# Low-rank terms of gate and up: from activations to the expanded weights

## What is computed

```python
def _lin_lora(x, W, A, B):
    base = jnp.einsum('bsh,oh->bso', x, W)
    lora = jnp.einsum('bsr,or->bso', jnp.einsum('bsh,rh->bsr', x, A), B)
    return base + lora
q, k, v = (_lin_lora(x, dequant(codes_attn[i], ...), lora_A_h[i], lora_B_attn[i]) for i in range(3))
attn = (q + k + v) / 3.0
x1 = x + _lin_lora(attn, dequant(codes_attn[3], ...), lora_A_h[3], lora_B_attn[3])
g = _lin_lora(x1, dequant(codes_gu[0], ...), lora_A_h[4], lora_B_gu[0])   # 1792 outputs
u = _lin_lora(x1, dequant(codes_gu[1], ...), lora_A_h[5], lora_B_gu[1])   # 1792 outputs
h = jax.nn.silu(g) * u
d = _lin_lora(h, dequant(codes_down, ...), lora_A_down, lora_B_down)
x = layernorm(x + x1 + d)
```

## Time and profile before

| | us |
|---|---|
| median of 3 runs | 562.48 (561.15 to 564.53) |
| the profiled execution's own time | 561.32 |
| its span on the core | 559.5 |
| TensorE busy | 495.7 (89%) |
| VectorE busy | 437.1 (78%) |
| ScalarE busy | 363.4 (65%) |
| GpSimd busy | 336.2 (60%) |
| mean granted clock | 0.966 |

### The profile page before, as it was taken

One profiled execution on the slowest core, in us unless ns is written; L12 is line 12 of the kernel. 1 busy time (PEld: TensorE's weight loads), 2 busy tenths in 40 slices (PEclk: granted clock), 3 DMA queues, 4 the chain that ended last, 5 costly groups with the idle time before them and its releaser, 6 DMA issues.

```text
span 559.5 us, 8029 instructions
## 1 busy us (share of the span) xinstructions
PE 495.7 (89%) x2246; PEld 399.0 (71%) x2246; DVE 437.1 (78%) x823; ACT 363.4 (65%) x657; POOL 336.2 (60%) x318
## 2 busy tenths in 40 slices
PE   0474549979799999999999999999999899999995
PEld 0152338767688888888888888778887688888874
DVE  7999988988868889999999999268646985555442
ACT  8999956688868578979889796126668541242121
POOL 5898824069866679989989899324649711010011
PEclk9996669989999999999999999999999999999999
DMA  8642402023322133333323230154000000010010
GB/s 268 247 147 75 132 19 68 15 89 134 97 90 77 57 94 105 104 95 111 116 94 114 94 100 15 56 198 151 2 1 1 1 2 1 19 39 21 0 39 37
DMA packets 20507, 43.70 MB, mean 78 GB/s; under 512 B 3312, under 2 KB 3440, under 8 KB 19952
## 3 DMA queue, kind: packets, MB, share of 16 engines
q1 hardware_dynamic: 20240, 42.81, 23.9%
q0 software_dynamic: 224, 0.38, 0.3%
HBM read 41.08 MB, written 2.10 MB: 77 GB/s over the span
## 4 chain that ended last, share of the span: by engine, by line
PE 68%; POOL 15%; issue 13%; ACT 2%; DVE 2%; POOLq 0%; ACTq 0%; DVEq 0%
PE bank L886 59%; POOL wf L623 6%; PE bank L1020 3%; POOL wf L631 3%; POOL wf L636 2%; PE bank L979 2%; POOL wf L642 2%; PE bank L1005 1%; PE bank L1124 1%; ACT prob L847 1%; ACT pT_hi L689 1%; PE bank L904 0%; DVE rmax L1335 0%; POOL wd_lo L649 0%; DVE pT_lo L1164 0%
## 5 line engine op out<-in xcount | busy, mean ns | idle before, releaser
L710 ACT ACTIVATE bank<-code 128x512 f32<-128x512 int32 x372 | 207.5, 594 | 18.7 <-DVE half L1183 7.7
L623 POOL TENSOR_TENSOR wf<-halves 128x512 f32<-128x512 f32 x62 | 80.2, 1294 | 69.3 <-DVE halves L1187 68.3
L886 PE MATMUL bank<-x_hi,gu_hi 128*128 128x512 f32 x224 | 88.4, 395 | 2.8 <-POOL gu_lo L649 2.2
L672 POOL TENSOR_TENSOR rstd<-veps,neg_half 128x1 f32<-128x1 f32 x32 | 17.7, 552 | 121.6 <-issue 110.4
L886 PE MATMUL bank<-x_hi,gu_lo 128*128 128x512 f32 x224 | 88.0, 393 | 0.0
L886 PE MATMUL bank<-x_lo,gu_hi 128*128 128x512 f32 x224 | 87.9, 392 | 0.0
L1183 DVE SCALAR_TENSOR_TENSOR half<-half,bank 128x512 f32<-128x512 f32 x124 | 81.2, 676 | 5.0 <-ACT bank L710 5.0
L1181 DVE SCALAR_TENSOR_TENSOR half<-code,bank 128x512 f32<-128x512 int32 x124 | 78.9, 676 | 5.2 <-ACT bank L710 3.8
L1187 DVE TENSOR_TENSOR halves<-half,bank 128x512 f32<-128x512 f32 x124 | 79.0, 677 | 0.0
L631 POOL TENSOR_TENSOR wf<-wf,scale 128x512 f32<-128x512 f32 x50 | 65.3, 1306 | 3.9
L886 PEld LDWEIGHTS bank<-x_hi,gu_hi 128*128 128x128 f32 x224 | 42.4, 189 | 12.3 <-issue 2.6
(11 more groups left out here) (199 smaller groups left out, 1130.5 us busy)
## 6 DMA issues: line engine op xcount, KB each, us to landing
code<-codes SPq DMA_DIRECT2D x62, 256.0 KB, 2.7
scale<-scales SPq DMA_DIRECT2D x100, 128.0 KB, 2.9
xs<-xT SPq DMA_DIRECT2D x1, 2048.0 KB, 11.8
ea_raw<-ex_A SPq DMA_DIRECT2D x1, 2048.0 KB, 9.7
eb_raw<-ex_B SPq DMA_DIRECT2D x1, 2048.0 KB, 7.7
out<-rows SPq DMA_DIRECT2D x8, 256.0 KB, 2.0
bgu_raw<-loB_gu SPq DMA_DIRECT2D x1, 1792.0 KB, 9.2
wqkv_raw<-w_qkv SPq DMA_DIRECT2D x1, 768.0 KB, 4.3
```

What stands on the lines that cost most here:

```text
L623: pool.tensor_tensor(w, halves[:, j % 2, 0, :], halves[:, j % 2, 1, :], ALU.subtract).then_inc(diff_done, 1)
L710: nc.scalar.activation(plane[m % RING_PLANE][:, :], src, func, bias=float(start), scale=float(slope)).then_inc(plane_ready, 1)
L886: last = nc.tensor.matmul(ps, a, b, start=start and i == 0 and n == 0, stop=stop and i == len(terms) - 1 and n == 2)
```

## The change

`MERGED` takes in the g and u chunks. For each of these TensorE makes the low-rank weight term A^T B as four matmuls of 128 moving columns (operands `la_gu` and `lb_gu`, float32r, with high and low parts stacked in the partitions), and VectorE adds it to `wf` ahead of the split, as for d chunks. The split of a g or u chunk is due after three halves where it was due after two. The product p, its two copies and splits, and the thirteenth matmul of each gate and up product go. The preparation of the operands is one high part of 128 x 1024 and one of 128 x 1792, with low parts over 32 partitions, where it was one of 128 x 512 and two of 128 x 1792; the transfers are 512 and 896 KB where they were 256 and 1792 KB. The orders of x1, of slice 0 and of TensorE's low-rank products are written anew: in TensorE's order of most slices f the product for the d chunk of f+1 is held back into the next slice, and those for g and u of f+1 stand behind the second and the third down product.

```diff
-MERGED = [c for c in CHUNKS if c[0] in "ovdf"]
+MERGED = [c for c in CHUNKS if c[0] not in "qk"]
...
-                due.append([3 if c in MERGED else 2, ("split", c)])
+                due.append([3, ("split", c)])
...
+    due.clear()
+    order += [("x1", 0), ("bprep", 0), ("x1", 1), ("bprep", 1), ("x1", 2)]
     half(("u", 0), 0)
-    order.append(("x1", 1))
+    order += [("x1", 3), ("merge", ("g", 0))]
     half(("u", 0), 1)
-    order += [("x1", 2), ("bprep", 0), ("x1", 3), ("bprep", 1), ("x1", 4), ("x1", 5), ("bprep", 2),
-              ("x1", 6), ("x1", 7)]
+    due.clear()
+    order += [("x1", 4), ("split", ("g", 0)), ("x1", 5), ("merge", ("u", 0)), ("x1", 6), ("split", ("u", 0)), ("x1", 7)]
     lut(("g", 1))
-    order.append(("p", 0))
     half(("u", 1), 0)
-    order.append(("p", 1))
...
 def tensor_order():
     order = []
+    held = ("d", 1)
     for f in range(NF):
-        downs = downs_beside(f)
+        downs = downs_beside(f) + [None] * 4
+        ahead = [(m, f + 1) for m in "gud"] if 1 <= f < NF - 1 else []
+        late = ("f", FFN_AT[f]) if f in FFN_AT else None
+        if f == 0:
+            beside = [None, ("u", 1), ("d", 0), None]
+        elif late:
+            beside = [ahead[0], ahead[1], ahead[2], None]
+        else:
+            beside = [held, *ahead[:2], None] if ahead else [held, None, None, None]
+        if late:
+            order.append(("lora", held))
         for b in range(NB):
             order.append(("gate", 2 * f + b))
-            if b == 0 and f < 2:
-                order.append(("lora", ("d", f)))
-            if b == 0 and f - 1 in FFN_AT:
-                order.append(("lora", ("f", FFN_AT[f - 1])))
-            order.extend(downs[2 * b:2 * b + 1])
+            if beside[2 * b] and not (late and b == 0) and not b:
+                order.append(("lora", beside[0]))
+            order.append(downs[2 * b])
+            if beside[2 * b] and (late and b == 0 or b):
+                order.append(("lora", beside[2 * b]))
             order.append(("up", 2 * f + b))
-            order.extend(downs[2 * b + 1:2 * b + 2])
-            if b == 0 and 1 <= f < NF - 1:
-                order.append(("lora", ("d", f + 1)))
+            order.append(downs[2 * b + 1])
+            if beside[2 * b + 1]:
+                order.append(("lora", beside[2 * b + 1]))
+        if f:
+            held = late or (ahead[2] if ahead else None)
     return order + downs_beside(NF)
...
-        bgu_raw = at("bgu_raw", 98, [P, 2, FF])
-        a4_raw = at("a4_raw", 112, [P, KT, P])
+        bgu_raw = at("bgu_raw", 98, [P, FF])
+        agu_raw = at("agu_raw", 105, [P, 2, 512])
...
-        bg4 = at("bg4", 134, [P, FF], F32R)
-        p4 = at("p4", 141, [P, TOK], F32R)
-        a4_hi = at("a4_hi", 205, [P, KT, P], F32R)
+        la_gu = at("la_gu", 134, [P, 2, 512], F32R)
...
                     act.wait_ge(bgu_in, 16)
-                    act.wait_ge(a4_in, 16)
+                    act.wait_ge(agu_in, 16)
                     act.wait_ge(weight_ready, 4 * KT)
-                    copy(*((a4_hi[:, :, :], a4_raw[:, :, :]), (bg4[:, :], bgu_raw[:, 0, :]),
-                           (bu4[:, :], bgu_raw[:, 1, :]))[i], bprep_hi)
+                    if i == 0:
+                        copy(la_gu[:, :, :], agu_raw[:, :, :], bprep_hi)
+                    else:
+                        copy(lb_gu[:, :], bgu_raw[:, :], bprep_hi)
...
-                elif kind == "p":
-                    b = item[1]
-                    act.wait_ge(p_ready, b + 1)
-                    copy(p4[:, b * SEQ:(b + 1) * SEQ], mm_ps[2 + b][:, :], phi_done)
...
+                elif kind in "gu":
+                    pe.wait_ge(bprep_done, 2)
+                    for h in range(KT):
+                        last = nc.tensor.matmul(lora_ps[:, h * P:(h + 1) * P],
+                                                la_gu[:, "gu".index(kind), h * P:(h + 1) * P],
+                                                lb_gu[:, k * P:(k + 1) * P], start=True, stop=True)
+                    last.then_inc(lora_ready, 1)
+                    return
...
-
-            pe.wait_ge(bprep_done, 3)
-            for b in range(NB):
-                pe.wait_ge(x1hi_done, NB * KT - 1 + b)
-                pe.wait_ge(x1lo_done, NB * KT - 1 + b)
-                pe.wait_ge(xs_done, NB * KT - 1 + b)
-                tk = slice(b * SEQ, (b + 1) * SEQ)
-                product(mm_ps[2 + b][:, :], [(a4_hi[:, k, :], a4_lo[:, k, :], x1_hi[:, k, tk], x1_lo[:, k, tk])
-                                             for k in range(KT)]).then_inc(p_ready, 1)
+                if n in (3, 5, 7):
+                    lora((("g", 0), ("u", 0), ("g", 1))[n // 2 - 1])
 
             def unit(n, g):
 
                 f, b = n // NB, n % NB
                 m = 2 * n + g
                 tk = slice(b * SEQ, (b + 1) * SEQ)
-                if m == 2:
-                    pe.wait_ge(phi_done, NB)
-                    pe.wait_ge(plo_done, NB)
+                if m <= 2:
+                    seen = (KT + 1, KT + 2, NB * KT)[m]
+                    pe.wait_ge(x1hi_done, seen)
+                    pe.wait_ge(x1lo_done, seen)
+                    pe.wait_ge(xs_done, seen)
                 elif m > 2 and g == 0:
                     pe.wait_ge(h_done, n - 1)
                 elif m > 2:
@@ -973,11 +978,7 @@
                 pe.wait_ge(lo_done, split_no(("gu"[g], f)))
                 s, ps = f % RING_GU, unit_ps[m % 3][:, :]
                 product(ps, [(gu_hi[:, s, g, k, :], gu_lo[:, s, g, k, :], x1_hi[:, k, tk], x1_lo[:, k, tk])
-                             for k in range(KT)], stop=False)
-                pe.wait_ge(phi_done, min(n + 1, NB))
-                pe.wait_ge(plo_done, min(n + 1, NB))
-                nc.tensor.matmul(ps, (bg4, bu4)[g][:, f * P:(f + 1) * P], p4[:, tk], start=False, stop=True)\
-                    .then_inc((gate_ready, unit_ready)[g], 1)
+                             for k in range(KT)]).then_inc((gate_ready, unit_ready)[g], 1)
 
...
-                    dve.wait_ge(low_rows_set, 4)
                     if i == 0:
-                        low(a4_lo[:, :, :], a4_raw[:, :, :], a4_hi[:, :, :], bprep_done)
+                        low(la_gu[32:64, :, :], agu_raw[32:64, :, :], la_gu[32:64, :, :], bprep_done)
                     else:
-                        b4 = (bg4, bu4)[i - 1]
-                        nc.vector.scalar_tensor_tensor(b4[:, :], b4[:, :].bitcast(F32), low_rows[:, 0:1],
-                                                       bgu_raw[:, i - 1, :], ALU.mult, ALU.add)\
-                            .then_inc(bprep_done, 1)
+                        low(lb_gu[64:96, :], bgu_raw[64:96, :], lb_gu[64:96, :], bprep_done)
...
-                elif kind == "p":
-                    b = item[1]
-                    tk = slice(b * SEQ, (b + 1) * SEQ)
-                    dve.wait_ge(phi_done, b + 1)
-                    low(p4[64:128, tk], mm_ps[2 + b][64:128, :], p4[64:128, tk], plo_done)
...
+    la_gu = np.zeros((P, 2, 512), np.float32)
+    lb_gu = np.zeros((P, FF), np.float32)
+    for i in range(3):
+        for g in range(2):
+            r = 32 * i + RANK * g
+            la_gu[r:r + RANK, g] = Ah[4 + g]
+            lb_gu[r:r + RANK] = Bg[g].T
```

More of the change, by code:

```diff
@@ L145, in vector_order @@
     half(("g", 0), 1)
-    order.append(("x1", 0))
+    due.clear()
+    order += [("x1", 0), ("bprep", 0), ("x1", 1), ("bprep", 1), ("x1", 2)]
     half(("u", 0), 0)
-    order.append(("x1", 1))
+    order += [("x1", 3), ("merge", ("g", 0))]
     half(("u", 0), 1)
-    order += [("x1", 2), ("bprep", 0), ("x1", 3), ("bprep", 1), ("x1", 4), ("x1", 5), ("bprep", 2),
-              ("x1", 6), ("x1", 7)]
+    due.clear()
+    order += [("x1", 4), ("split", ("g", 0)), ("x1", 5), ("merge", ("u", 0)), ("x1", 6), ("split", ("u", 0)), ("x1", 7)]
     lut(("g", 1))
-    order.append(("p", 0))
     half(("u", 1), 0)
-    order.append(("p", 1))
     order.append(("dprep", 0))
@@ L305, in build @@
         lb_qkv = at("lb_qkv", 192, [3 * RANK, 512])
-        bu4 = at("bu4", 194, [P, FF], F32R)
+        lb_gu = at("lb_gu", 194, [P, FF], F32R)
         la_d = at("la_d", 30, [P, FF // 2])
@@ L311, in build @@
         lb_dhi = at("lb_dhi", 82, [P, 2, 512], F32R)
-        a4_lo = at("a4_lo", 132, [P, KT, P], F32R)
         ident = at("ident", 207, [P, P])
@@ L395, in build @@
         bgu_in = sem("bgu_in")
-        a4_in = sem("a4_in")
+        agu_in = sem("agu_in")
         plane_ready = sem("plane_ready")
@@ L421, in build @@
         fprep_done = sem("fprep_done")
-        p_ready = sem("p_ready")
-        phi_done = sem("phi_done")
-        plo_done = sem("plo_done")
         gate_ready = sem("gate_ready")
@@ L559, in _ @@
                 if c == ("k", 1):
-                    sp.dma_start(bgu_raw[:, :, :], loB_gu).then_inc(bgu_in, 16)
-                    sp.dma_start(a4_raw[:, :, :], loA_gu).then_inc(a4_in, 16)
+                    sp.dma_start(bgu_raw[:, :], loB_gu).then_inc(bgu_in, 16)
```

(18 more changed lines are left out.)

## The result

The changed kernel is slower: a median of 579.18 us (577.32 to 579.87, four runs) against 561.82 (560.74 to 564.53, four runs) for the kernel before, a ratio of 1.0296 with a 95% interval from 1.025 to 1.0342. The forecast was 573.0 us. The direction came as forecast, and so did most of the mechanisms. The size did not: +17.4 us where I had +11.7.

A forecast was written before the change was run, and what follows sets the result against it. The prediction took TensorE to bound slices 4 to 12, with VectorE nearly full, and chunk expansion up to slice 2. Front +1.0, splits of u +1.2 and +0.5, slices 6 to 13 +9.0 took 561.3 to 573.0 us, range 566 to 580.

The forecast's parts named there:

- my own case: Whole kernel: the main forecast of 573.0 us, chance 0.62, with its own range from 569 to 577.
- The bound moves to VectorE: Slices 5 to 12: with two more additions a slice, VectorE's pair of slices takes 36.7 us against TensorE's 35.1.
- The 128 columns at 0.111 us: TensorE's new float32r matmuls of 128 columns cost 0.111 us each, eight making 0.89 us a slice.
- The rival of dear 128 columns: TensorE pays 128 columns like 512, 0.227 us each, giving 578.4 us; chance 0.14.
- My 35.1 us for TensorE's pair: Slices 5 to 12: TensorE's work in a pair of slices, set against VectorE's 36.7 us.
- Four VectorE additions at 0.598: Pair of slices: two new VectorE additions a slice at 0.598 us each, on 34.3 us of work before.
- Slice 6 at +2.7: Slice 6 takes 20.2 us, TensorE waiting 1.4, 0.2 and 0.9 us for VectorE's additions; slice 12 alone adds +2.7.
- Slice 7: 17.7 us, without a wait worth a tenth: Slice 7: VectorE waits for the first down product but has the slack, so the pair is 37.9 us.
- The split of u: One half later, behind the split of h: +1.2 us at up(4) in slice 2, +0.5 in slice 5.
- The front: Up to slice 2: gate(0) 4.2 us earlier, TensorE idle 8 us, start of slice 2 at +1.0 us.
- The rival that buffers hide the waits: Slices 6 to 12: buffers hide the waits and only the work counts, +5.4 us, giving 566.7; chance 0.15.
- the faster one: Slice 2 starts 4.2 us early with TensorE, and additions fit VectorE's idle time, giving 556.2 us; chance 0.06.

The follow-up runs named there:

- E1: Changed kernel without TensorE's low-rank products for g and u chunks and their waits, VectorE keeping one 128 x 512 instruction for each: 568.90 us.
- e5: Changed kernel with the identity addition of the four f chunks done by GpSimd instead of VectorE: 575.65 us.
- E4: Changed kernel with TensorE's products for chunks moved to where VectorE's previous addition is already made, no work added or removed: 573.12 us.
- e3: Changed kernel with the split of a u chunk put ahead of the split of h where both fall due at one half: 575.24 us.
- e10: Changed kernel with TensorE's product for u1 moved behind gate(1) and that for d0 behind up(1): 578.55 us.
- e8: Kernel before with TensorE's low-rank product for d0 behind gate(1) in place of gate(0): 562.05 us, ratio 0.9986.
- e11: Changed kernel with products spread, split of u first, identity addition on GpSimd and u1's product behind gate(1): 565.60 us.
- e2: Changed kernel with VectorE's addition for g and u chunks cut to one column, products, places and waits kept: 569.69 us.
- e6: Changed kernel with low-rank products moved later in slices 0 and 1, u1's behind up(1), d0's behind gate(2): 581.48 us.

## Why the forecast was right, and where it fell short

The 579.18 lies near the upper end of my range (566 to 580), and outside the 569 to 577 that I gave my own case. So the direction and the sum's terms are confirmed one by one below, but that the range held it is in part luck.

**The bound moves to VectorE: right.** E1 shows it by itself.

**The 128 columns at 0.111 us: right.** The rival of dear 128 columns gave 578.4, nearest to the result, by a price that the trace refutes. A time alone would have confirmed the wrong mechanism. My 35.1 us for TensorE's pair doesn't agree with my own two slices of 17.67 and 17.7; with 0.45 for each chunk it is 35.3, which changes no step, for TensorE was not the slower one.

**Four VectorE additions at 0.598: right, their base too small.** I had 36.7 us of VectorE work in a pair and it was 37.5. The additions themselves were near; the window of the same pair of before already holds 34.84 where I had counted 34.3. The identity addition, which I had at 0.2 us, costs 0.80 by its timeline and 0.9 by e5.

**Slice 6 at +2.7: right, with smaller waits.** The slice took 20.0 us (225.99 to 245.99) where I had 20.2, against 17.45 before:

```profile
231.37 0.66 PE L905 MATMUL bank<-lb_gu,la_gu 128*128 128x128 f32 x4 [0.76 <-DVE wf L1198]
236.15 0.66 PE L905 MATMUL bank<-lb_gu,la_gu 128*128 128x128 f32 x4
241.53 0.50 PE L914 MATMUL bank<-lb_dp,la_dp 128*128 128x512 f32 x1 [0.56 <-DVE wf L1198]
```

By the starts 0.92, 0.13 and 0.72 us stand ahead of the g, u and d products, where I had 1.4, 0.2 and 0.9. The 0.7 that this falls short of my 2.5 is mostly made up by the longer places behind the breaks, which I did not have.

**"Slice 7: 17.7 us, without a wait worth a tenth": this step failed.** The slice took 18.95 us (245.99 to 264.94). My figure rested on VectorE's slack, 36.7 of 37.9. With 37.5 there is too little for its wait of 1.48 us, which I had named and called absorbed: the wait comes on top, 37.5 + 1.5 = 39.0. The delay then reaches TensorE in slice 7 too, 0.73 us ahead of the u product (260.16), which waits for the addition of the g term, and 0.17 ahead of the g product. I had taken the longer of the two engines where each handed its delay to the other. E4 takes the handing away and leaves the work (37.43), e5 takes the work away and leaves the handing (38.02). In slices 6 to 12 this is 2.8 of the 6.5 us by which the span exceeded the forecast.

**The split of u: right (+1.4 for 1.2), but not its price at the clock.** In slice 5 the wait for u's low part came too, 0.56 us by the starts where I had 0.5. The rest of the +1.1 of slices 3 to 5 is some 0.1 us at each of six products of 128 columns, which took 0.47 to 0.49 us where I had 0.39. I had bounded the low clock in the front alone, and its price there a little high: behind the wait at 116.86 nine matmuls took 3.64 us (118.09 to 121.73), which is 1.6 us lost and not 1.8. The second stretch, behind up(4), I had at nothing. It cost 1.7 us, and e3 removed it along with the wait.

**The front: mostly cover, as forecast.** Gate(0) came at 107.89 (forecast: near 107), TensorE idled 6.9 us (8), and slice 2 began at 145.10 (near 144). E1, e10 and e8 show that all but about 1 us of the idle time is free. Of the +2.0, some 1.3 us comes from far ahead of it: VectorE's eighth low-rank addition starts at 75.18 where it did at 73.87. In both traces TensorE waits for the first low-rank operand's transfer at the start, first before, then after:

```profile
PE bank L913 <- DMA lb_qkv<-loB_qkv: 14.2, 1, 14.2
```

```profile
PE bank L923 <- DMA lb_qkv<-loB_qkv: 15.6, 1, 15.6
```

The transfer itself is unchanged. In e8, a form of the kernel before, it took 15.0 us, and in the eleven traces of changed forms 12.7 to 16.6, the shortest in e11:

```profile
PE bank L927 <- DMA lb_qkv<-loB_qkv: 12.7, 1, 12.7
```

So it varies by 4 us between traces, and both traces of the kernel before lie within that range. These 1.3 us are no effect of the change that the runs can show.

The rival that buffers hide the waits (566.7) fell with e2 and e4, whose waits or places alone are worth 1.5 to 1.7 us of a pair, and the faster one with slice 2's start.

## What to carry to other kernels

When a change brings a second engine to the load of the first, don't take the longer of the two: follow a whole period in both, and ask of each wait whether the other engine has slack left to absorb it, for with none the waits add. Count such an engine's work from a window of the real period, not from instructions by a mean, since a few small dependent ones decide it. A product that feeds the fuller engine belongs where what it waits for is already done, still ahead of its consumer, and behind nothing that waits (e6 had it behind such a wait). Moving the products to better places was worth 6 us here with no work removed.

## What the runs showed of the hardware

The length of an idle stretch of TensorE does not by itself say which clock follows. Before, 2.18 us of waiting at 143.10 was followed by full clock (1.00) in each window of 1 us up to 149. After, 2.04 us at 150.33 was followed by 0.53 and 0.50 in the windows from 151, and TensorE had been idle for 0.81, 1.37 and 0.28 us at 136.53, 141.36 and 145.10. The fall came some 0.7 us after the work had resumed. In e3 the wait there was 0.79 us behind almost the same idle stretches (0.81, 1.39, 0.30), and the clock stayed at 1.00.

A VectorE addition of a quarter of the columns can cost more than a full one: 128 x 128 took 0.80 us from start to start behind the instruction that it depends on, the independent 128 x 512 ones 0.60. On GpSimd its record is 0.46 us. Whether the dependence or the shape makes it dear was not tested.
